# Where the products with the values stand in TensorE's order: two steps in each of two quarters, or four steps at the end of the last

## The reference, cut to what matters

```python
q = einsum('bsm,hmd->bhsd', x, kernel[0]); k, v likewise with kernel[1], kernel[2]
scores = einsum('bhsd,bhtd->bhst', q, k) * scale
attn = softmax(scores, axis=-1)
out = einsum('bhst,bhtd->bhsd', attn, v)
out = out.transpose(0, 2, 3, 1).reshape(b, s, d * h) @ WO[0]
```

## Time and profile before

| | |
|---|---|
| median of 3 runs | 3794.4 us (3791.53 to 3797.76) |
| profiled execution | 3790.69 us |
| its span, first to last instruction | 3788.9 us |
| busy in the span: PE / DVE / ACT / POOL | 95% / 59% / 44% / 69% |
| mean granted clock of TensorE | 0.981 |

### The profile page before, as it was taken

The page is one execution under the profiler, slowest core; times in us unless marked ns, Lnnn a source line. Parts: engine busy times, 40 slices in busy tenths (PEclk is TensorE's granted clock), DMA queues, the critical chain, the costliest instruction groups (busy, mean ns, idle before and its releaser), DMA issues. The chain is left out here.

```text
span 3788.9 us, 61436 instructions
## 1 busy us (share of the span) xinstructions
PE 3597.7 (95%) x17248; PEld 2334.3 (62%) x17248; DVE 2246.7 (59%) x2976; ACT 1676.7 (44%) x3216; POOL 2624.2 (69%) x1467
## 2 busy tenths in 40 slices
PE   3999999999999999997986999999999999999799
PEld 3566666666666666656873565656565656665488
DVE  4544444444444444445766777777777777777354
ACT  2444444444444444444543444444444444444354
POOL 2677777777777777773333787888788878887521
PEclk9999999999999999998997999999999999999899
DMA  6433443344334434411115345444544454443100
GB/s 201 94 80 78 111 89 78 77 111 86 78 81 100 92 78 89 89 40 33 45 56 103 82 87 106 86 86 86 106 85 86 86 107 86 86 86 78 37 18 28
DMA packets 423700, 313.74 MB, mean 83 GB/s; under 512 B 258848, under 2 KB 296608, under 8 KB 422560
## 3 DMA queue, kind: packets, MB, share of 16 engines
q1 hardware_dynamic: 415616, 286.78, 36.0%
q10 hardware_dynamic: 7968, 25.69, 2.1%
HBM read 88.35 MB, written 21.50 MB: 29 GB/s over the span
## 5 line engine op out<-in xcount | busy, mean ns | idle before, releaser
L925 POOL TENSOR_TENSOR a_rs<-a_rs,a_p 128x1024 f32<-128x1024 f32 x384 | 917.2, 2388 | 338.8 <-ACT a_p L831 321.3
L925 POOL TENSOR_TENSOR b_rs<-b_rs,b_p 128x1024 f32<-128x1024 f32 x384 | 916.8, 2387 | 268.4 <-ACT b_p L831 250.9
L851 DVE TENSOR_REDUCE a_nmax<-a_ps_x 128x1 fp32r<-128x1024 f32 x508 | 622.3, 1225 | 775.3 <-PE a_ps_x L631 771.7
L851 DVE TENSOR_REDUCE b_nmax<-b_ps_x 128x1 fp32r<-128x1024 f32 x508 | 622.3, 1225 | 363.2 <-PE b_ps_x L631 355.7
L831 ACT ACTIVATE a_p<-a_ps_s 128x512 f32<-128x512 f32 x1024 | 529.6, 606 | 419.9 <-PE a_ps_s L647 419.7
L831 ACT ACTIVATE b_p<-b_ps_s 128x512 f32<-128x512 f32 x1024 | 529.6, 606 | 351.9 <-PE b_ps_s L647 345.3
L663 PE MATMUL b_ps_o<-b_p,b_v 128*64 128x512 f32 x2048 | 467.7, 598 | 0.0
L663 PE MATMUL a_ps_o<-a_p,a_v 128*64 128x512 f32 x2048 | 467.7, 598 | 0.0
L646 PE MATMUL b_ps_s<-b_q,b_k 128*128 128x512 f32 x1024 | 416.9, 407 | 2.0 <-DMA b_q<-b_nmax 1.4
L646 PE MATMUL a_ps_s<-a_q,a_k 128*128 128x512 f32 x1024 | 415.2, 405 | 1.9 <-DMA a_q<-a_nmax 1.1
L647 PE MATMUL b_ps_s<-b_q,b_k 128*128 128x512 f32 x1024 | 402.8, 393 | 0.0
(11 more groups left out here) (171 smaller groups left out, 5491.9 us busy)
## 6 DMA issues: line engine op xcount, KB each, us to landing
a_q<-a_nat_h SPq DMA_DIRECT2D x250, 128.0 KB, 2.4
a_k<-a_nat_h SPq DMA_DIRECT2D x250, 128.0 KB, 2.4
b_q<-b_nat_h SPq DMA_DIRECT2D x250, 128.0 KB, 3.3
b_k<-b_nat_h SPq DMA_DIRECT2D x250, 128.0 KB, 3.4
a_rinv<-rows_a SPq DMA_DIRECT2D x128, 128.0 KB, 2.9
b_rinv<-rows_b SPq DMA_DIRECT2D x128, 128.0 KB, 3.4
a_q<-a_nat_l SPq DMA_DIRECT2D x125, 128.0 KB, 2.4
a_k<-a_nat_l SPq DMA_DIRECT2D x125, 128.0 KB, 2.4
```

The lines of the kernel that those rows point to most:

```text
L851: dve.reduce_max(nmax[:, g % 2, head, qi:qi + 1], max_banks(t, c)[:, 0:2, :].rearrange("p a b -> p (a b)"), AX_X, negate=True).then_inc(s_ ...
L925: pool.tensor_tensor(out, out, p[:, bb, i, :], ALU.add).then_inc(s_sum, 1)
```

## The change

In the first attention (`rope` is None) `values` leaves quarters 0 and 2. All four steps of group `u` are issued in one run in quarter 3 of the group's own window, behind `out_project`. `row_sums` stays in quarter 2 and so follows `maxima(c+1)`, or `project_v` where there is one. The second attention keeps its order. The number of instructions and every wait in `values` are the same.

```diff
                 w = {0: u - 1, 2: u}.get(b)
-                if w is not None and live(t, 4, w, NGROUP):
+                if rope is not None and w is not None and live(t, 4, w, NGROUP):
                     values(pe, t, w, 2 - b)
                     values(pe, t, w, 3 - b)
+                if rope is None and b == 3 and live(t, 4, u, NGROUP):
+                    for step in range(4):
+                        values(pe, t, u, step)
                 if b == 2 and live(t, 4, u - 1, NGROUP):
                     row_sums(pe, t, u)
```

## The result

The changed kernel takes 3901.8 us (median of 4 runs, 3898.6 to 3905.4) against 3796.1 us; the ratio is 1.0287 with a 95% interval of 1.0275 to 1.0299, some 109 us by the ratio and 106 by the two medians. The forecast was 3890 us, slower; the range 3868 to 3915 holds it.

The account below looks back on a forecast made before the run. TensorE, busy 95% of the span and almost never waiting, was taken as the bound. Fifteen bodies 82.8, first quarter 0 2.2, last body 1.2, feature loads 8.0 and low clock 2 made 96 us: 3890 us, range 3868 to 3915.

Parts of the forecast that it names:

- Quarters 0 and 2 without project_v: Windows 0 and 1: maxima to maxima becomes 1.95 us, waiting for DVE's reduction; quarters 2.19 and 2.77 us shorter.
- The list of what would show it: Signs in the profile after, among them maxima waiting for a_nmax over 90 times, some 80 to 110 us.
- The rival of the hidden reduction: Steady loop: reduction overlaps its matmuls, 1.2 us not 1.95, 92 stretches lose 69 us less, 3820; chance 0.05.
- With project_v: Windows 2 and 3: quarter 0 3.62 us shorter; quarter 2 waits for ACT's second copy, 3.38 us, 2.76 shorter.
- Quarter 3: Where the values go: run of thirty-two takes 7.02 us, 7.05 with its entry, bounds 7.0 to 7.16.
- its count of turns: Changes into and out of the values' tiling: 0.23 us a group, 64 of them gaining 15 us.
- Feature loads and the clock: Reader in quarter 3 comes 2.77 us earlier: three waits, +8.0 us; low clock after them, +2 us.
- the first and last bodies: Very first quarter 0 already had its wait, +2.2 us; the last body, without project_v, +1.2 us.
- The clock did not fall at the repeated waits: Rival: clock falls at repeated short waits; about 3940 with quarter 0's 30 waits, 4040 with quarter 2's 62; chance 0.07.
- `out_project` did not become late: Rival: a later step, out_project in quarter 3, becomes late; 1 us in 62 windows gives 3950; chance 0.04.
- The rival *faster: Turns of the values' tiling cost over 1.5 us a group; at 1.8, 3775 us; chance 0.02 for faster or no change.
- POOL fell nowhere behind: Held to be free: POOL has 338.8 us idle before its additions in this attention, so it falls behind nowhere.

Follow-up runs that it names:

- q0_only: Only steps 2 and 3 of the values move from quarter 0 to quarter 3, against the kernel before; 3847.4 us, ratio 1.0136.
- q2_only: Only steps 0 and 1 of the values move from quarter 2 to quarter 3, against the kernel before; 3867.8 us, ratio 1.0197.
- half_reduce_new: The changed kernel with DVE's maximum in the first attention over 512 of the 1024 keys; 3869.3 us, ratio 1.0195 to the kernel before.
- values_first: The changed kernel with the run of 32 values ahead of out_project in quarter 3, not behind it; 3906.6 us, ratio 1.0306 to the kernel before.
- half_features: The changed kernel with only 512 of 1024 positions loaded in the first attention's three feature loads; 3889.4 us, ratio 1.0259 to the kernel before.
- rows_in_ps_o: The changed kernel with the first attention's row sums written to the values' bank ps_o; 3886.1 us, ratio 1.0244 to the kernel before.

## Why the prediction was right, and what it mis-sized

**The place of the loss.** TensorE hardly ever waited in this stage, so each wait that the new order made was paid in full. `q0_only`, `q2_only` and the two kernels with a shorter reduction show it from both sides.

**Quarters 0 and 2 without project_v.** 2.19 and 2.77 us shorter were forecast from a stretch of 1.95; it is 1.94, over 30 times each. Right. The list of what would show it was not: it has over 90 waits for `a_nmax` and 80 to 110 us, and there are 68 with 69.7 us. The prediction's own sum has only some 64 such waits; 92 takes in the 30 stretches of quarter 2 that end on the copy of `v_next`. The rival of the hidden reduction has the same slip: 0.75 us in 64 stretches is 48 us, about 3840 and not 3820.

**With project_v.** Quarter 0 hides the reduction, quarter 2 waits for the copy of `v_next`: 3.38 us forecast and measured, 30 waits of 0.75 us. Right.

**Quarter 3: the term that was too small.** I took 7.05 us for the run with its entry. The run is 7.02, its entry takes 0.28 more than the `maxima` that stood there, and the `maxima` pair behind it 0.07 less (0.57 us from its start to the scores, where it was 0.65, 809.51 to 810.16 above): 7.23. That is 0.18 us in 62 windows, 11 us. What was too small was the price of the turn, in and out. Take the time from the start of the block ahead to the next scores, once with the values and once without, and subtract the 0.43 us of each pair of values: what is left is the turn, and it is nearly the same in four places (medians, us):

| values between | with | without | pairs | turn |
|---|---|---|---|---|
| `project_v` and `maxima`, before | 5.67 | 1.90 (`half_reduce_new`, no wait) | 3.43 | 0.34 |
| `out_project` and `maxima`, changed | 8.55 | 1.32 | 6.87 | 0.36 |
| `project_qk` and `out_project`, `values_first` | 9.94 | 2.72 | 6.87 | 0.35 |
| `out_project` and `maxima`, `q0_only` | 5.12 | 1.32 | 3.43 | 0.36 |

The prediction had 0.17 of it in quarter 3 (0.14 at the end of the run and 0.03 for the entry) and 0.23 in its count of turns. It left out that the `maxima` pair behind the values takes 0.57 us, where one with neither a wait nor another tiling ahead takes 0.47, and took less than the 0.09 of the entries that it had seen. The Trainium skill ("TensorEngine Tiling (Array Packing)", Key Properties) says that a change of mode drains the engine. The trace agrees in kind: the values' first weight load starts with their first matmul, 0.31 us after the start of `out_project`'s last, where a full-array load starts with it. Why the price splits differently between way in and way out at different neighbours is not shown.

**Feature loads and the clock.** Forecast 8.0 us of waits and 2 of low clock. Measured: 10.1 us of waits, since the three transfers landed 10.4, 11.0 and 11.5 us after their issue and not 10.1 to 10.7, and 13.7 us at 1.2 GHz, at most 6.8 us. The three windows are 16.5 us too long together; this term was short by about 6. Not all that is beyond the waits is the clock's: in `half_features`, at full clock and with 2.1 us of waits, they are still 3.8 us too long.

**The sum.** Forecast 96, the profile has 111 in this stage. A body without a feature load loses 6.15 us and not 5.5, which makes 9 in 15 bodies: 11 of turns, less 1 to 2 because quarters 0 and 2 got some 0.01 us shorter each than forecast. The features make 6; the first and last bodies are within 1 us. The 3.7 us behind the stage were in no term. Both misses go the same way, so the forecast was not saved by errors that cancel.

**The rivals.** The clock did not fall at the repeated waits: in the 1688 us of `half_features` it stays at 1.00. What the Trainium skill tells of short idles between groups of matmuls ("TensorE: Matmul & The Clock Gate", A second HAM failure mode) does not show here at 62 waits of up to 1.3 us. `out_project` did not become late in the windows. No part of the 1.95 us was hidden. The rival *faster* wanted a turn worth over 1.5 us; it is worth 0.35. POOL fell nowhere behind; its idle before L928 went from 338.8 to 117.9 us and moved to the group's first addition, L924, which shows 336.2 (26 before).

**A version better than both?** None of the runs points to one. The new order allows `row_sums` in `ps_o`, but even with that a window loses. By the rows, every stretch that the values left needs some 1.5 us of other work for TensorE (1.94 less the pair's 0.47). Windows 0 and 1 have no `project_v`; whether `project_qk` could stand there was not tried.

## What to carry to other kernels

On an engine that never waits, a block's place is also a cover: before moving it, find for each pair of neighbours that will now touch what the second waits for from the first, and look in the trace (first and last iterations are good places) for a spot where they touch already. Price a change of tiling from the block ahead to the block behind, with and without the run: starts at one border alone show only part of it. A big transfer that is "just in time" is a wait as soon as anything ahead of its reader gets shorter.

## What the runs showed of the hardware

- A reduction of 1024 float32 columns from PSUM took 1.22 us and one of 512 took 0.69; a matmul that waited for it started 0.05 to 0.06 us after its end, 68 times.
- A run of matmuls on 64 columns of the array between full-array matmuls cost 0.34 to 0.36 us beyond its own pairs, in and out together, whether it was 16 or 32 instructions long and whichever of three blocks stood ahead of it.
- TensorE's granted clock went to 1.2 GHz, for 3.4 or 6.8 us, at each of 15 waits for features of 2.0 to 4.1 us (three each in the changed kernel, `q2_only`, `half_reduce_new`, `values_first` and `rows_in_ps_o`), and at none of the 62 waits of up to 1.3 us in `half_features`.
